# Weights stored by input channel instead of turned on TensorE, and a new order of the first two images

## The chip, the cores and the metric

One core of a Trainium2 chip runs the program. The metric is the device time of one execution in microseconds. The host's preparation of the inputs is not in it.

## What is computed

x is (8, 512, 32, 48) in float32, there are 40 centroids, W is 512 x 512.

```python
xn = x / max(norm(x, axis=1), EPS); cn = centroids / max(norm(centroids, axis=1), EPS)
idx = argmax(einsum('bchw,nc->bnhw', xn, cn), axis=1)          # nearest of 40 centroids
onehot = one_hot(idx, 40)
sum_x = einsum('bhwn,bchw->bnc', onehot, x)                     # cluster sums of each image
centroids_local = sum_x / max(count, 1)
gathered = centroids_local[b, idx]                              # mean of the pixel's cluster
delta = gathered - x
alpha = exp(-mean(delta * delta, axis=1))
y = x + alpha * delta
out = relu(einsum('oc,bchw->bohw', W, y) + b)
```

## The kernel before

An image has 1536 pixels, cut into three units of 512 pixels; units 0 to 23 run through the eight images. Channels are four blocks of 128 on the partitions. Each engine has its own program, written out by hand in order, and semaphores tie them together. Nothing reorders an engine's program: what stands behind a waiting instruction waits too.

For each unit `similarities(g)` (L915) multiplies x by the centroids. The result goes through ScalarE (`copy_sims`, L712) back to TensorE, `transpose_sims` (L924), and VectorE finds the maximum and the one-hot of all three units of an image in five instructions (`best_sims` and `first_best`, L425 to L440). `sum_clusters(b, u)` (L960) multiplies the one-hot by x with pixels on the partitions (the tile `xt`). `add_halves` (L970, L972) and a few small steps make the means G. `gather(g, h)` (L1000) multiplies the means by the one-hot, `delta(g, h)` (L483, VectorE) subtracts x, `square` (L673, ScalarE) squares, `add_chunks` adds the four channel blocks (for units 0 and 1 on GpSimd, L382 twice and L385 once), `sum_squares_direct(g)` (L1011) sums over partitions, `exp` (L688), `scale` (L519, VectorE, with `al` in PSUM), `y_half` (L527 on VectorE for unit 0, L360 on GpSimd for most others; both operands in SBUF), a high and a low part of y (L693, L367) and the product with the weights in three passes, `convolve` (L1023 to L1025; `high_passes`, L1084, for unit 0). The product of a unit comes two units after its gather.

x with pixels on the partitions comes in three ways. For image 1 (units 0 to 2) TensorE transposes it (`transpose_x`, L1037, 8 transposes of 128 x 128 a half unit) into the PSUM banks `gat` and `main`, and ScalarE (once VectorE) copies it out, `keep_transposed` (L655). Units 4 and 5 of image 2 are turned in the same way by `turn(step)` (L1055) and `keep_turned(step)` (L662); `TURNS` lists the steps and their tiles. All other units are loaded a second time as blocks of 32 channels (`load_xs`, L275, four loads a unit) and turned by VectorE, `transpose_half` (L411).

The weights are loaded once into the output buffer `OUT[0]` (L292). TensorE transposes them, `transpose_weights(k)` (L1077, 4 transposes each), into `gat` and `main`; `high_weights(k)` (L781, ScalarE) and `low_weights(k)` (L539, VectorE) split them into two parts. The squares of unit 0 use `OUT[0]` afterwards.

All loads and stores are issued by one queue, SP, in the order of its program. In what follows unit and image numbers are counted from 0 in the code; the text's "image 2" is b = 1, units 3 to 5.

Of the kernel before, what the change touches and what calls it, by code (L numbers as in the profile page):

```python
# [14 lines left out]
P = 128  # L15
# [27 lines left out]
TURNS = ((PARTS + 1, (0,)), (PARTS + 1, (1,)), (PARTS + 1, (2, 3)), (PARTS + 2, (0, 1)), (PARTS + 2, (2, 3)))  # L43
# [55 lines left out]
def build(nc, x, cent, w, bias, out):  # L99
# [3 lines left out]
    with ctx:  # L103
# [48 lines left out]
        cstat = sb("cstat", [P, 7], F32)  # L152
        Wraw = OUT[0]
# [31 lines left out]
        wT_ps, wh_done, wl_done = sem("wt_ps"), sem("wh_done"), sem("wl_done")  # L185
# [23 lines left out]
        def wT(k):  # L209
            return (gat[:, 0, :], gat[:, 1, :], main[:, 0, :], main[:, 1, :])[k]  # L210
# [51 lines left out]
        def _(sp):  # L262
# [33 lines left out]
            load_x(4)  # L296
            load_x(5)
            load_xs(3)
# [99 lines left out]
        def _(dve):  # L398
# [165 lines left out]
            low_weights(0)  # L564
            low_weights(1)
            low_clusters(0)
            counts(0)
            low_weights(2)
            rest_of_mean(0)
            parts_of_mean(0)  # L570
            low_weights(3)

            delta(0, 0)
            delta(0, 1)
            transpose_half(3, 0)
# [4 lines left out]
            transpose_half(3, 1)  # L580
# [69 lines left out]
        def _(act):  # L650
# [14 lines left out]
            def square(g, h):  # L665
                act.wait_ge(z_done, 2 * g + h + 1)
                if g < LAG:

                    act.wait_ge(wT_ps, KC)
                    act.wait_ge(const_done, 7)  # L670
                elif h == 0:
                    wait(act, s_done, folded(g - 1))
# [106 lines left out]
            def high_weights(k):  # L779
                act.wait_ge(wT_ps, k + 1)  # L780
# [3 lines left out]
            copy_sims(1)  # L784
            keep_transposed(0, 1)
            copy_sims(2)
# [4 lines left out]
            high_weights(0)  # L791
            high_weights(1)
            copy_onehot(0)
            copy_sums(0)
            evacuate_onehot()
            high_weights(2)
            scale_means(0)
            high_means(0)
            high_weights(3)
            keep_turned(0)  # L800
            act.wait_ge(b_in, 16)
            copy_sims(3)
            copy_sims(4)
# [3 lines left out]
            keep_turned(1)  # L807
            keep_turned(2)
            keep_turned(3)
            keep_turned(4)  # L810
# [81 lines left out]
        def _(pe):  # L892
# [43 lines left out]
            def sum_clusters(b, u):  # L936
# [4 lines left out]
                if PARTS * b + u in TURNED:  # L941
                    pe.wait_ge(xe_act, KEPT + 3 + 2 * TURNED.index(PARTS * b + u))
# [32 lines left out]
            def gather(g, h):  # L975
# [3 lines left out]
                if g == 0:  # L979

                    pe.wait_ge(wl_done, KC // 2 * (h + 1))
                    if h == 0:
                        pe.wait_ge(xe_act, KEPT + 1)
                elif g < LAG:

                    pe.wait_ge(xe_act, KEPT + 4 + h)
# [54 lines left out]
            def turn(step):  # L1041
                g, tiles = TURNS[step]
                if step == 0:

                    pe.wait_ge(wl_done, 1)
                elif step < 3:

                    pe.wait_ge(z_done, step)
                else:

                    pe.wait_ge(xe_act, KEPT + step - 1)
# [21 lines left out]
            def transpose_weights(k):  # L1073
# [124 lines left out]
```

## Time and profile before

| | us |
|---|---|
| median of 3 runs | 410.63 (409.59 to 411.04) |
| the profiled execution | 410.88 |
| its span, first to last instruction | 409.1 |
| TensorE busy | 403.9 |
| VectorE busy | 338.9 |
| GpSimd busy | 262.1 |
| ScalarE busy | 260.7 |
| granted TensorE clock | 0.999 |

The span is 1.8 us shorter than the execution. Times in the rows are from the span's start. TensorE's matmuls are pipelined, so a row's duration overlaps the next by 0.1 to 0.2 us; the chain of waits shows pieces without overlap.

### The profile page before, as it was taken

What the parts mean: (1) busy time and instruction counts of PE and PEld (TensorE: products, weight loads), DVE (VectorE), ACT (ScalarE), POOL (GpSimd) and SP (SyncE); (2) the same over time, 40 slices, a digit from 0 to 9 for tenths busy, and PEclk for the clock granted to TensorE, in tenths of its full rate; (3) what the DMA queues carried; (4) which work ended last, traced back from release to release, by engine and by line L of the source; (5) the groups of instructions that cost most, each with busy time, mean ns of one, the idle gap of its engine ahead of it and who ended that gap; (6) DMA issues with size and microseconds to landing.
All of it is one profiled execution on the core that took longest, in us unless ns stands there. A gap on an engine that the chain in (4) does not pass through costs nothing.

```text
span 409.1 us, 5812 instructions
## 1 busy us (share of the span) xinstructions
PE 403.9 (99%) x2088; PEld 288.2 (70%) x2088; DVE 338.9 (83%) x415; ACT 260.7 (64%) x362; POOL 262.1 (64%) x117
## 2 busy tenths in 40 slices
PE   8999999999999999999999999999999999999997
PEld 5746376775867677775867758776777758777886
DVE  2439999888899879999799898998799897898730
ACT  6566783767665684665865576656846658676641
POOL 2003773984599676994789946996769947433420
PEclk9999999999999999999999999999999999999999
DMA  7992493988499395967979575994957240222213
GB/s 256 380 248 51 88 244 84 297 252 180 172 246 266 113 281 140 272 162 183 265 198 229 191 163 188 254 256 118 276 139 226 104 129 13 103 103 104 103 68 138
DMA packets 77918, 74.51 MB, mean 182 GB/s; under 512 B 13723, under 2 KB 52891, under 8 KB 77891
## 3 DMA queue, kind: packets, MB, share of 16 engines
q1 hardware_dynamic: 77890, 74.15, 64.7%
q8 instruction: 17, 0.28, 0.3%
q14 instruction: 11, 0.08, 0.1%
HBM read 46.22 MB, written 25.17 MB: 174 GB/s over the span
## 4 chain that ended last, share of the span: by engine, by line
PE 95%; POOL 1%; DMA 1%; ACT 1%; issue 0%; DVE 0%; SPq 0%; ACTq 0%
PE main L1023 21%; PE main L1024 21%; PE main L1025 21%; PE fa L915 11%; PE sump L960 8%; PE gat L1000 5%; PE fa L924 1%; PE al L1006 1%; DMA x<-x 1%; PE main L1084 1%; PE main L1037 1%; PE al L1011 1%; POOL o L382 1%; POOL o L385 1%; PE gat L1037 1%; PE main L1055 0%
## 5 line engine op out<-in xcount | busy, mean ns | idle before, releaser
L1023 PE MATMUL main<-yh,wh 128*128 128x512 f32 (+1 forms) x376 | 152.8, 406 | 0.0
L1024 PE MATMUL main<-yl,wh 128*128 128x512 f32 (+1 forms) x376 | 146.3, 389 | 0.0
L1025 PE MATMUL main<-yh,wl 128*128 128x512 f32 (+1 forms) x376 | 146.1, 389 | 0.0
L360 POOL TENSOR_TENSOR z<-z,x 128x1024 f32<-128x1024 f32 x41 | 97.4, 2395 | 60.5 <-DVE z L519 60.5
L367 POOL TENSOR_TENSOR yl<-z,yh 128x1024 fp32r<-128x1024 f32 x43 | 103.7, 2429 | 13.8 <-ACT yh L693 13.7
L701 ACT ACTIVATE o<-main,bcol 128x512 f32<-128x512 f32 x96 | 65.1, 680 | 46.8 <-PE main L1025 45.9
L1023 PEld LDWEIGHTS main<-yh,wh 128*128 128x128 f32 x376 | 70.7, 188 | 21.4 <-issue 4.6
L1025 PEld LDWEIGHTS main<-yh,wl 128*128 128x128 f32 x376 | 70.6, 188 | 14.9
L1024 PEld LDWEIGHTS main<-yl,wh 128*128 128x128 f32 x376 | 70.7, 188 | 13.8
L374 POOL TENSOR_TENSOR xr<-xt 128x2048 f32<-128x2048 f32 x11 | 51.5, 4684 | 19.1 <-DVE xt L411 19.1
L483 DVE TENSOR_TENSOR z<-gat,x 128x1024 f32<-128x1024 f32 x46 | 55.8, 1213 | 6.1 <-PE gat L1000 6.1
L519 DVE TENSOR_TENSOR z<-z,al 128x1024 f32<-128x1024 f32 x48 | 56.3, 1210 | 0.6 <-ACT al L688 0.5
L693 ACT ACTIVATE yh<-z 128x1024 fp32r<-128x1024 f32 x48 | 50.6, 1053 | 3.6 <-POOL z L360 1.8
L915 PE MATMUL fa<-x,c_t 128*64 128x256 f32 x384 | 47.2, 394 | 0.5 <-DMA x<-x 0.5
L411 DVE STREAM_TRANSPOSE xt<-xs 128x1024 f32<-128x1024 f32 x38 | 46.1, 1225 | 0.0
L915 PEld LDWEIGHTS fa<-x,c_t 128*64 128x64 f32 x384 | 26.5, 140 | 19.3 <-issue 5.8
L673 ACT ACTIVATE sq<-z 128x1024 f32<-128x1024 f32 x21 | 22.3, 1060 | 25.7 <-DVE z L483 25.7
L673 ACT ACTIVATE gat<-z 128x1024 f32<-128x1024 f32 x21 | 21.5, 1024 | 25.2 <-DVE z L483 25.2
L419 DVE TENSOR_TENSOR xr<-xr 128x2048 bf16<-128x2048 f32 x11 | 36.7, 3338 | 0.2
L960 PE MATMUL sump<-xt,oh 128*64 128x512 f32 (+1 forms) x148 | 31.7, 537 | 0.0
L382 POOL TENSOR_TENSOR o<-o 128x512 f32<-128x512 f32 x4 | 5.1, 1284 | 36.2 <-ACT o L673 36.2
L1000 PE MATMUL gat<-oht,g 128*128 128x512 bf16 x92 | 27.8, 384 | 0.0
(139 smaller groups left out, 402.6 us busy)
## 6 DMA issues: line engine op xcount, KB each, us to landing
out<-o SPq DMA_DIRECT2D x23, 1024.0 KB, 7.2
x<-x SPq DMA_DIRECT2D x21, 1024.0 KB, 6.6
xs<-x SPq DMA_DIRECT2D x76, 256.0 KB, 5.5
x<-x SPq DMA_DIRECT2D x12, 256.0 KB, 5.4
o<-w SPq DMA_DIRECT2D x1, 1024.0 KB, 8.4
out<-o SPq DMA_DIRECT2D x3, 256.0 KB, 2.0
out<-o SPq DMA_DIRECT2D x2, 128.0 KB, 1.7
oht<-oh SPq DMA_TRANSPOSE x7, 3.7
```

Source lines behind the costliest of these rows:

```text
L360: pool.tensor_tensor(z, z, X[g // PARTS % 2][:, pair(h), span(g)], ALU.add).then_inc(y_pool, 1)
L367: pool.tensor_tensor(YL[g % 2][:, pair(h), :], Z[g % 2][:, pair(h), :], YH[g % 2][:, pair(h), :].bitcast(F32), ALU.subtract).then_inc(lo_p ...
L374: pool.tensor_tensor(XR[:, g % PARTS, :, :].rearrange("p t c -> p (t c)"), xt.rearrange("p t c -> p (t c)"), halfword(xt, 1), ALU.subtract ...
L483: v_.tensor_tensor(Z[g % 2][:, pair(h), :], banks(g, h)[:, :, :], X[g // PARTS % 2][:, pair(h), span(g)], ALU.subtract).then_inc(z_done, 1)
L519: v_.tensor_tensor(z, z, al[:, :].unsqueeze(1).to_broadcast([P, 2, UNIT]), ALU.mult).then_inc(za_done, 1)
L693: a_.activation(YH[g % 2][:, pair(h), :], Z[g % 2][:, pair(h), :], ACT.Copy).then_inc(hi_done, 1)
L701: a_.activation(OUT[g % 2][:, o, cols], main[:, o % 2, cols], ACT.Relu, bias=bcol[:, o:o + 1]).then_inc(relu_done, 1)
L915: last = t_.matmul(simP[u][NPAD * h:NPAD * (h + 1), :], cT[:, k, :], toks, start=(k == 0), stop=(k == KC - 1))
L960: last = t_.matmul(sumP[NPAD * h:NPAD * (h + 1), :], onehot[:, slot(u, tile), :], x_part[:, tile * C:(tile + 1) * C], start=(opens and t = ...
L1023: t_.matmul(tile, WH[:, k, rows], YH[g % 2][:, k, cols], start=(k == 0), stop=False)
L1024: t_.matmul(tile, WH[:, k, rows], YL[g % 2][:, k, cols], start=False, stop=False)
L1025: last = t_.matmul(tile, WL[:, k, rows], YH[g % 2][:, k, cols], start=False, stop=(k == KC - 1))
```

## The change

The host stores W transposed, so that what lands in `OUT[0]` is already laid out by input channel. `transpose_weights` goes, `wT(k)` names the landed rows, `high_weights` waits for the load itself, and its four calls move on ScalarE: the first stands between two evacuations of x. On TensorE the similarities of unit 2 move ahead of `transpose_x(0, 1)`, `transpose_sims(0)` ahead of `transpose_x(1, 0)`. The five turning steps become four of two tiles each, two of them ahead of the first gather. `sum_squares_direct(0)` moves behind `gather(1, 1)`. VectorE does the two halves of unit 3's transposes before and after the first two deltas, instead of later. SP loads unit 3's blocks ahead of unit 5.

```diff
-TURNS = ((PARTS + 1, (0,)), (PARTS + 1, (1,)), (PARTS + 1, (2, 3)), (PARTS + 2, (0, 1)), (PARTS + 2, (2, 3)))
+TURNS = ((PARTS + 1, (0, 1)), (PARTS + 1, (2, 3)), (PARTS + 2, (0, 1)), (PARTS + 2, (2, 3)))
...
         def wT(k):
-            return (gat[:, 0, :], gat[:, 1, :], main[:, 0, :], main[:, 1, :])[k]
+            return Wraw[:, k, :]
...
             load_x(4)
+            load_xs(3)
             load_x(5)
-            load_xs(3)
             load_xs(6)
...
             first_best(0)
-            low_weights(0)
-            low_weights(1)
+            for k in range(KC):
+                low_weights(k)
             low_clusters(0)
             counts(0)
-            low_weights(2)
             rest_of_mean(0)
             parts_of_mean(0)
-            low_weights(3)
-
+
+            transpose_half(3, 0)
             delta(0, 0)
             delta(0, 1)
-            transpose_half(3, 0)
+            transpose_half(3, 1)
             best_sims(1)
             first_best(1)
             delta(1, 0)
             delta(1, 1)
-            transpose_half(3, 1)
             scale(0, 0)
...
                 if g < LAG:
 
-                    act.wait_ge(wT_ps, KC)
+                    act.wait_ge(wl_done, KC)
...
             def high_weights(k):
-                act.wait_ge(wT_ps, k + 1)
+                act.wait_ge(w_in, 16)
                 a_.activation(WH[:, k, :], wT(k), ACT.Copy).then_inc(wh_done, 1)
...
-                if g == 0:
-
-                    pe.wait_ge(wl_done, KC // 2 * (h + 1))
-                    if h == 0:
-                        pe.wait_ge(xe_act, KEPT + 1)
-                elif g < LAG:
-
-                    pe.wait_ge(xe_act, KEPT + 4 + h)
+                if g < LAG:
+
+                    pe.wait_ge(xe_act, KEPT + 2 * g + h + 1)
...
-                if step == 0:
-
-                    pe.wait_ge(wl_done, 1)
-                elif step < 3:
-
-                    pe.wait_ge(z_done, step)
+                if step < 2:
+
+                    pe.wait_ge(xe_act, KEPT - 1 + step)
                 else:
 
-                    pe.wait_ge(xe_act, KEPT + step - 1)
+                    pe.wait_ge(z_done, step - 1)
...
-            def transpose_weights(k):
-                pe.wait_ge(w_in, 16)
-                pe.wait_ge(xe_act, 4 if k < 2 else 5)
-                for o in range(KC):
-                    last = t_.transpose(wT(k)[:, o * P:(o + 1) * P], Wraw[:, o, k * P:(k + 1) * P], ident[:, :])
-                last.then_inc(wT_ps, 1)
...
-        "w": np.ascontiguousarray(L0_conv_W),
+        "w": np.ascontiguousarray(np.asarray(L0_conv_W).T),
```

Where the instructions stand now. TensorE from the second similarities to the cluster sums of image 1, before (`x` is the image, `fa`, `gat` and `main` are PSUM banks, `o` the landed weights):

```order
L915 MATMUL fa<-x,c_t 64x256 x8
L1037 MATMUL main<-ident,x 128x128 x8
L915 MATMUL fa<-x,c_t 64x256 x8
L1037 MATMUL gat<-ident,x 128x128 x8
L924 MATMUL fa<-ident,sims 128x128 x6
L1037 MATMUL main<-ident,x 128x128 x8
L1037 MATMUL gat<-ident,x 128x128 x8
L1037 MATMUL main<-ident,x 128x128 x8
L1077 MATMUL gat<-ident,o 128x128 x8
L960 MATMUL sump<-xt,oh 64x512 x12
```

and after, where the same lines have other numbers:

```order
L913 MATMUL fa<-x,c_t 64x256 x16
L1030 MATMUL main<-ident,x 128x128 x8
L922 MATMUL fa<-ident,sims 128x128 x6
L1030 MATMUL gat<-ident,x 128x128 x8
L1030 MATMUL main<-ident,x 128x128 x8
L1030 MATMUL gat<-ident,x 128x128 x8
L1030 MATMUL main<-ident,x 128x128 x8
L958 MATMUL sump<-xt,oh 64x512 x12
```

The two similarities stand together, the transposed similarities come two steps sooner, and the eight weight transposes are gone.

TensorE from the first gather to the cluster sums of image 2, before:

```order
L1000 MATMUL gat<-oht,g 128x512 x2
L1000 MATMUL main<-oht,g 128x512 x2
L915 MATMUL fa<-x,c_t 64x256 x8
L1055 MATMUL gat<-ident,x 128x128 x4
L924 MATMUL fa<-ident,sims 128x128 x6
L1055 MATMUL main<-ident,x 128x128 x8
L1055 MATMUL gat<-ident,x 128x128 x8
L1055 MATMUL main<-ident,x 128x128 x8
L1000 MATMUL gat<-oht,g 128x512 x2
L1011 MATMUL al<-o,ones 128x512
L1000 MATMUL main<-oht,g 128x512 x2
L960 MATMUL sump<-xt,oh 64x512 x12
```

and after:

```order
L993 MATMUL gat<-oht,g 128x512 x2
L993 MATMUL main<-oht,g 128x512 x2
L913 MATMUL fa<-x,c_t 64x256 x8
L1045 MATMUL gat<-ident,x 128x128 x8
L922 MATMUL fa<-ident,sims 128x128 x6
L1045 MATMUL main<-ident,x 128x128 x8
L993 MATMUL gat<-oht,g 128x512 x2
L993 MATMUL main<-oht,g 128x512 x2
L1004 MATMUL al<-o,ones 128x512
L958 MATMUL sump<-xt,oh 64x512 x12
```

Twelve of the tile transposes now stand ahead of the first gather, and the sum of squares comes behind both gathers of unit 1.

VectorE from the argmax of image 2 to the y of unit 0, before:

```order
L440 TENSOR_TENSOR oh<-rank,fa 128x12x40
L483 TENSOR_TENSOR z<-gat,x 128x1024
L483 TENSOR_TENSOR z<-main,x 128x1024
L411 STREAM_TRANSPOSE xt<-xs 128x8x4x32
L519 TENSOR_TENSOR z<-z,al 128x1024
L527 TENSOR_TENSOR z<-z,x 128x1024
L519 TENSOR_TENSOR z<-z,al 128x1024
L527 TENSOR_TENSOR z<-z,x 128x1024
```

and after:

```order
L441 TENSOR_TENSOR oh<-rank,fa 128x12x40
L484 TENSOR_TENSOR z<-gat,x 128x1024
L484 TENSOR_TENSOR z<-main,x 128x1024
L520 TENSOR_TENSOR z<-z,al 128x1024
L528 TENSOR_TENSOR z<-z,x 128x1024
L520 TENSOR_TENSOR z<-z,al 128x1024
L528 TENSOR_TENSOR z<-z,x 128x1024
```

The block transpose between the deltas and the first scale is gone from here.

## Rows read from the trace of the kernel before

**Rows 1.** The page, part 4: the chain that ended last, shares by engine.
```profile
PE 95%; POOL 1%; DMA 1%; ACT 1%; issue 0%; DVE 0%; SPq 0%; ACTq 0%
```

**Rows 2.** TensorE's waits: total us, times, longest us.
```profile
PE al L1011 <- POOL o L385: 0.3, 1, 0.3
```

**Rows 3.** The chain, first 80 us: start us, us, engine, tile, line, count.
```profile
14.96 1.02 PE gat L1037 x8
15.99 0.66 PE fa L924 x6
...
17.55 1.03 ACT xt L655
...
18.63 1.10 PE main L1037 x8
19.73 0.97 PE gat L1077 x8
20.70 5.32 PE sump L960 x24
...
28.66 0.43 PE gat L1055 x4
...
33.70 1.88 PE fa L915 x16
...
36.16 0.86 PE fa L924 x6
```

**Rows 4.** Timeline, 40 to 48 us, all engines: start, us, engine, line, tiles, [idle before].
```profile
40.65 1.23 DVE L483 TENSOR_TENSOR z<-gat,x 128x1024 f32<-128x1024 f32 x1 [0.16 <-PE gat L1000]
...
41.94 1.22 DVE L483 TENSOR_TENSOR z<-main,x 128x1024 f32<-128x1024 f32 x1
...
42.00 2.26 ACT L673 ACTIVATE o<-z 128x1024 f32<-128x1024 f32 x2
...
43.13 2.53 POOL L382 TENSOR_TENSOR o<-o 128x512 f32<-128x512 f32 x2 [3.39 <-ACT o L673]
...
44.24 1.18 DVE L519 TENSOR_TENSOR z<-z,al 128x1024 f32<-128x1024 f32 x1
45.46 1.28 DVE L527 TENSOR_TENSOR z<-z,x 128x1024 f32<-128x1024 f32 x1
...
45.73 2.15 POOL L385 TENSOR_TENSOR o<-o 128x512 f32<-128x512 f32 x1
...
47.90 1.23 DVE L527 TENSOR_TENSOR z<-z,x 128x1024 f32<-128x1024 f32 x1
47.90 3.50 POOL L367 TENSOR_TENSOR yl<-z,yh 128x1024 fp32r<-128x1024 f32 x1
```

**Rows 5.** Timelines of GpSimd and of VectorE at 122 us.
```profile
121.89 2.39 POOL L367 TENSOR_TENSOR yl<-z,yh 128x1024 fp32r<-128x1024 f32 x1
124.24 5.97 POOL L374 TENSOR_TENSOR xr<-xt 128x2048 f32<-128x2048 f32 x1
...
122.59 4.20 DVE L419 TENSOR_TENSOR xr<-xr 128x2048 bf16<-128x2048 f32 x1
```

**Rows 6.** Timeline of SP's queue: issues of weights, unit 5, unit 3's fourth block.
```profile
7.33 0.53 SPq L292 DMA_DIRECT2D o<-w  x1
...
12.09 1.22 SPq L268 DMA_DIRECT2D x<-x  x1
...
21.30 1.30 SPq L275 DMA_DIRECT2D xs<-x  x1
```

**Rows 7.** DMA issues at 6.8, 7.3, 12.1, 21.3 us: KB each, us from issue to landing.
```profile
x<-x SPq DMA_DIRECT2D x1, 256.0 KB, 6.1
...
o<-w SPq DMA_DIRECT2D x1, 1024.0 KB, 8.4
...
x<-x SPq DMA_DIRECT2D x1, 1024.0 KB, 13.6
...
xs<-x SPq DMA_DIRECT2D x1, 256.0 KB, 9.4
```

More of the change, by code:

```diff
@@ L184, in build @@
         cT_ps, cT_done, norm_step = sem("ct_ps"), sem("ct_done"), sem("norm_step")
-        wT_ps, wh_done, wl_done = sem("wt_ps"), sem("wh_done"), sem("wl_done")
+        wh_done, wl_done = sem("wh_done"), sem("wl_done")
         xp_done, xe_dve, xe_act = sem("xp_done"), sem("xe_dve"), sem("xe_act")
@@ L784, in _ @@
             copy_sims(1)
+            copy_sims(2)
             keep_transposed(0, 1)
-            copy_sims(2)
+            high_weights(0)
             keep_transposed(1, 0)
@@ L790, in _ @@
             keep_transposed(2, 1)
-            high_weights(0)
             high_weights(1)
             copy_onehot(0)
+            high_weights(2)
+            high_weights(3)
             copy_sums(0)
             evacuate_onehot()
-            high_weights(2)
             scale_means(0)
             high_means(0)
-            high_weights(3)
             keep_turned(0)
@@ L802, in _ @@
             copy_sims(3)
+            keep_turned(1)
             copy_sims(4)
@@ L806, in _ @@
             square(0, 1)
-            keep_turned(1)
             keep_turned(2)
             keep_turned(3)
-            keep_turned(4)
             exp(0)
@@ L941, in sum_clusters @@
                 if PARTS * b + u in TURNED:
-                    pe.wait_ge(xe_act, KEPT + 3 + 2 * TURNED.index(PARTS * b + u))
+                    pe.wait_ge(xe_act, KEPT + 2 + 2 * TURNED.index(PARTS * b + u))
                 elif b > 0:
@@ L1089, in _ @@
             similarities(1)
+            similarities(2)
             transpose_x(0, 1)
-            similarities(2)
+            transpose_sims(0)
             transpose_x(1, 0)
-            transpose_sims(0)
             transpose_x(1, 1)
@@ L1096, in _ @@
             transpose_x(2, 1)
-            transpose_weights(0)
-            transpose_weights(1)
             pe.wait_ge(const_done, 7)
@@ L1103, in _ @@
             transpose_onehot()
-            transpose_weights(2)
-            add_halves(0)
-            transpose_weights(3)
             pe.wait_ge(x_in[1][1], 16)
             turn(0)
+            add_halves(0)
+            turn(1)
             similarities(3)
@@ L1113, in _ @@
             similarities(5)
-            turn(1)
+            turn(2)
             transpose_sims(1)
-            turn(2)
             turn(3)
-            turn(4)
             gather(1, 0)
+            gather(1, 1)
             sum_squares_direct(0)
-            gather(1, 1)
             sum_clusters(1, 1)
@@ L1127, in _ @@
             pe.wait_ge(z_done, 4)
+            pe.wait_ge(wl_done, KC)
             pe.wait_ge(hi_done, 1)
```

## The prediction

> **What bounds the kernel now.** Read the chain of waits first: TensorE carries 95% of the span [rows 1]. Then the list of TensorE's own waits: it is short, and its last entry in time is 0.3 us in front of `sum_squares_direct(1)`, for GpSimd's last chunk sum [rows 2], whose matmul starts at 48.01. After that TensorE waits for nothing to the end, so whatever shift `sum_squares_direct(1)` has is the shift of the whole kernel. The change lies entirely ahead of that point. The question is therefore not how many matmuls go, but when that one instruction starts. I walk the first 48 us engine by engine, in order, with the durations of the rows; each instruction keeps the order that the changed program gives it.
>
> **Removed: the 16 weight transposes (L1077).** Eight cost 0.97 us on the chain at 19.73; four fill the 0.44 from 28.22 to the row at 28.66 [rows 3]. The other four lie in the stretch in which TensorE waits for the high and low parts of the cluster sums, so they cost nothing. That is 1.41 us on the chain. The four copies of weight rows on ScalarE and the four subtractions on VectorE remain, with SBUF as the source in place of PSUM. I take the same 0.6 and 0.7 us for them. Except for the first one on ScalarE they fall into the 5.32 us of `sum_clusters(0, *)` [rows 3], where both engines have room. If SBUF made them twice as long they would still end about when `sum_clusters` does, at 25. The new waits for the low weights (first square on ScalarE, `high_passes` on TensorE) come 9 us and more after that and cost nothing.
>
> **Moved: the similarities of unit 2 ahead of `transpose_x(0, 1)`.** They start at 12.06 instead of 13.09. Their last slice of x, issued at 6.8, lands 6.1 us later at 12.9 [rows 7]. It is wanted at 12.06 plus three quarters of 1.9, so 13.5. No wait. They end at 13.94, the transposes of x at 14.98, and `transpose_sims(0)` at 15.64 where it was 16.65 (the row at 15.99 and its 0.66) [rows 3]. VectorE's argmax follows about 1.0 earlier.
>
> **Added: `high_weights(0)` in front of `keep_transposed(1, 0)` on ScalarE.** `keep_transposed(0, 1)` starts at 15.02 when its transposes end and takes 1.03 like its sister at 17.55 [rows 3]; ScalarE can take the next at about 15.95, a little before it ends. The weights are issued at 7.33 and land 8.4 later, at 15.7 [rows 6, 7], just before. The copy delays the next evacuation by 0.48. That evacuation ends at 17.60, and `transpose_x(2, 0)`, which refills the bank, starts at 17.64. Before, the last pair of x transposes waited for ScalarE in the same way and started at 18.63 [rows 3]. Now TensorE runs 1.10 + 0.97 from 17.64 and begins `sum_clusters` at 19.71, where it began at 20.70: **0.99 earlier**. So 0.97 of transposes gone, and the 1.0 of the reordering spent again on ScalarE.
>
> **Moved: the turned tiles of image 2.** `turn(0)` and `turn(1)` (8 transposes each, 0.93 and 0.90) now stand before and after `add_halves(0)`. `sum_clusters` and the one-hot transposes end at 25.69, `turn(0)` at 26.62. Before, `add_halves` (0.7) ended at 28.22, so it started at 27.52, 1.5 after the end of `sum_clusters` at 26.02, because its inputs came then; now they come at 25.03 + 1.5 = 26.5, and the turn covers it. `add_halves` and `turn(1)` end at 28.22. Before, the similarities of unit 3 began when the row at 28.66 ended, 29.10 [rows 3]: 0.88 earlier. From 29.10 to 36.16 TensorE did similarities, two gathers, the last similarities (1.88 from 33.70) and four tile transposes, 7.06 us [rows 3]. Now there are eight tile transposes in place of four, 0.37 more (0.95 against 0.58). Then six transposes at 0.68, which before took 0.86 since ScalarE's copy came late; the free ones at 15.99 took 0.66 [rows 3]. They end at 36.33 against 37.02: **0.69 earlier**. Twelve tile transposes of the 32 leave the stretch behind this point, so TensorE itself gains 1 us more there; VectorE does not.
>
> **Moved: unit 3's blocks.** The fourth block load of unit 3 is issued at 21.30 and lands at 30.7; unit 5, in front of it, is issued at 12.09 and lands at 25.7 [rows 6, 7]. Unit 5 is wanted by `similarities(5)`, 0.88 before the 33.70 of rows 3. The gathers begin 1 us before that, at 31.8, and `transpose_half(3, 0)` stands on VectorE between the means and the deltas, so it wants the blocks at about 31.4. In the new order the two exchange places: blocks at about 28, unit 5 at about 30.7. Both have 2 us or more. The transpose costs VectorE 0.1 us against `delta(0, 0)`, which has 1 us of room before `turn(2)` needs it.
>
> **The step that decides.** The argmax of image 2 ends 3.47 us after the transposed similarities (37.02 to 40.49, where VectorE went idle for 0.16) [rows 3, 4], so now at 39.80, and `delta(1, 0)` starts there: 0.85 earlier than 40.65. `delta(1, 1)` follows at 40.94, `scale(0, 0)` at 42.08 (steps of 1.14, as from 41.94 through the block transpose to 44.24, and that transpose is gone), `y_half(0, 0)` 1.22 later at 43.30 [rows 4]. ScalarE's square starts 0.02 after the delta's 1.23 and takes 1.06, so GpSimd's first chunk sum of unit 1 runs from 42.18 to 43.46. The second, 1.27, would run to 44.73 and the third to 46.1. `sum_squares_direct(0)`, moved behind `gather(1, 1)`, is done before the argmax is, so its move costs nothing. TensorE arrives at `sum_squares_direct(1)` at 45.76 (it starts `sum_clusters(1, 1)` at 39.90, when the one-hot is there, and 5.32 + 0.54 follow), so it would run at 46.2: the gain would be 1.8.
>
> The trace says that GpSimd does not run freely beside this VectorE instruction. The third chunk sum took 2.15 instead of 1.27. It was to start at 45.73, while `y_half(0, 0)` ran from 45.46; 45.46 + 1.28 = 46.74, and 46.74 + 1.14 = 47.88, its end [rows 4]. `y_half(0, 1)` and the low half on GpSimd both began at 47.90; VectorE took 1.23, GpSimd 3.50 instead of 2.39, which is again VectorE's end plus a run [rows 4, 5]. While VectorE scaled by a PSUM operand (44.24) GpSimd lost nothing. And when VectorE waits behind one GpSimd instruction and another stands right behind it, VectorE goes between: L419 issued at 122.59 waited for the end of L367 at 124.28, and L374, issued at 124.24, ended at 130.21, 3.4 after L419's end at 126.79 [rows 5].
>
> With that in the walk: `y_half(0, 0)` waits for 43.46 and ends at 44.54; the second sum ends at 45.68; `scale(0, 1)` from 44.46; `y_half(0, 1)` wants the port at 44.46 + 1.24 = 45.70, the third sum at 45.68 + 0.07 = 45.75. VectorE is ahead by 0.05 and runs to 46.93; the third sum ends at 48.07; TensorE starts 0.12 later at 48.19. **That is 0.18 us later than 48.01**: all that the change removes is waited for again, 2.4 us long, at `sum_squares_direct(1)`.
> The Trainium skill (SBUF — State Buffer, Who interferes with whom) says of a VectorE instruction with two SBUF inputs and a GpSimd instruction that reads SBUF that whichever is issued first has the port for all of its run. The rows agree, and by that rule too the order 45.70 before 45.75 decides; with the order turned round the time would be the second case below.
>
> **Sum.** Span 409.1 + 0.18 = 409.3. The profiled execution took 410.88, 0.25 above the median of 410.63; on the median's footing the forecast is **410.8**. Behind `sum_squares_direct(1)` every wait hangs on ScalarE's exp, which hangs on it, so the pattern moves as a whole.
>
> **Rivals.**
> (B) GpSimd gets one of the two turns. My walk is good to about 0.1 us, and the margins are 0.16 and 0.05. Then the third sum ends at 46.95 (43.46 + 1.27, 1.08 of VectorE, 1.14), TensorE at 47.1: 0.9 earlier, 409.7. For it: the thin margin. Against it: rows 4 show the same race at 47.90 with VectorE winning.
> (C) The removed work comes through whole: TensorE at 46.2, 408.8. It takes a GpSimd that is not held up at all; two rows speak against it.
> (D) Slower: the weights land late. ScalarE stands in order at `high_weights(0)`, with four evacuations of x behind it that TensorE waits for. From a landing at 16.0 on, each us of lateness is one us for TensorE. Other 1 MB loads of this queue land up to 13.6 after issue [rows 7] instead of 8.4; with a latency of 10.4, 2 us more, the weights come at 17.7 and the kernel is at about 412.5. Against it: nothing ahead of them in the queue changes.
> (E) The change doesn't do what it says on the clock because unit 5 lands late: pushed behind the blocks it may mix with unit 6's and come at 33 to 34; one us late is one us, about 411.8.
>
> **Chances.** The forecast 0.52, B 0.20, C 0.13, D 0.08, E 0.07. A measurement of this kernel can tell about 0.3% (1.2 us) from no change. Faster by more: C and a third of B and a little of the forecast, 0.23. Slower by more: D, half of E and a little of the forecast, 0.14. Within: 0.63. The range 409.0 to 412.2 leaves out C and the far end of D, and holds the spread of the runs.
>
> **What would show it.** TensorE's waits: `sum_squares_direct(1)` for GpSimd, about 2.4 us (forecast), 1.3 (B), 0.4 (C). The chunk sums of unit 1: second and third over 2 us each (forecast), one of them (B), none (C). `sum_clusters(0, 0)` starting at 19.7; if it starts later, a wait of ScalarE for the weights (D). The similarities of unit 5 waiting for a DMA (E). The forecast is wrong if TensorE waits less than 1 us in front of `sum_squares_direct(1)`.

## The result: slower by 0.6%, and the profile after

| | before | after |
|---|---|---|
| median of 20 executions, us | 410.44 | 412.90 |
| lowest to highest, us | 409.59 to 411.05 | 410.62 to 416.83 |
| after / before, 95% interval | | 1.0062 (1.0049 to 1.0075) |
| profiled execution, us (its span) | 410.88 (409.1) | 412.77 (411.0) |
| executions with a mean granted clock below 0.999 | 0 of 20 | 14 of 20 |

The forecast was 410.8 in a range of 409.0 to 412.2, with "within 0.3%" the likeliest. The median lies 2.1 us above the forecast and outside the range, on the side that I gave 14 in 100. The spread has changed too: before, all executions lie within 1.5 us of each other, after, within 6.2.

The list of TensorE's waits of the profiled execution of after (total us, times, longest us), which answers to [rows 2]:

```profile
PE al L1004 <- POOL o L386: 2.2, 1, 2.2
PE fa L913 <- DMA x<-x: 1.5, 1, 1.5
PE al L1052 <- POOL ones L335: 1.0, 1, 1.0
PE gat L1030 <- ACT xt L654: 0.9, 1, 0.9
PE main L993 <- ACT xt L661: 0.6, 1, 0.6
```

The first is the wait that the forecast names, at `sum_squares_direct(1)` (L1004). The second is rival E, the similarities of unit 5. The third is the start and was there before. The chain that ended last has lost seven points of TensorE against [rows 1] to SP's queue and the DMAs, which is unit 5's way into the chip:

```profile
PE 88%; SPq 5%; DMA 3%; POOL 1%; DVE 1%; issue 0%; ACT 0%
```

The same execution in its timeline, 16 to 50 us, TensorE, VectorE, ScalarE and GpSimd mixed (start, us, engine, line, tiles, idle before and who ended it). These rows answer to [rows 3, 4]:

```profile
16.44 0.63 ACT L780 ACTIVATE wh<-o 128x512 fp32r<-128x512 f32 x1 [0.61 <-DMA o<-w]
18.04 1.09 PE L1030 MATMUL gat<-ident,x 128*128 128x128 f32 x8 [0.86 <-ACT xt L654]
19.98 5.37 PE L958 MATMUL sump<-xt,oh 128*64 128x512 f32 x24
28.36 3.67 PE L913 MATMUL fa<-x,c_t 128*64 128x256 f32 x32
34.55 1.95 PE L913 MATMUL fa<-x,c_t 128*64 128x256 f32 x16 [1.55 <-DMA x<-x]
41.56 1.22 DVE L484 TENSOR_TENSOR z<-gat,x 128x1024 f32<-128x1024 f32 x1
...
43.95 3.51 POOL L383 TENSOR_TENSOR o<-o 128x512 f32<-128x512 f32 x2 [3.29 <-ACT o L672]
45.07 1.25 DVE L528 TENSOR_TENSOR z<-z,x 128x1024 f32<-128x1024 f32 x1
46.24 1.21 DVE L520 TENSOR_TENSOR z<-z,al 128x1024 f32<-128x1024 f32 x1
47.48 1.22 DVE L528 TENSOR_TENSOR z<-z,x 128x1024 f32<-128x1024 f32 x1
47.54 2.29 POOL L386 TENSOR_TENSOR o<-o 128x512 f32<-128x512 f32 x1
49.88 1.12 PE L1004 MATMUL al<-o,ones 128*128 128x512 f32 x2 [2.21 <-POOL o L386]
```

Read the lower half first, since it is the step on which the forecast was built. From `delta(1, 0)` to `sum_squares_direct(1)` the walk had 39.80 to 48.19, 8.39 us; the trace has 41.56 to 49.88, 8.32. GpSimd's first two chunk sums of unit 1 took 3.51 together, where the pair took 2.53 before [rows 4]: the second was held up. The third took 2.29: it stands behind `y_half(0, 1)` (47.48), which came 0.06 us before the third sum's start (47.54); the walk said 0.05. The whole of it stands 1.7 us later than forecast, and 1.55 of that is the wait at 34.55 for unit 5. The span of this execution, 411.0, is the forecast's 409.3 plus the same 1.7. So the profiled execution has one fault of the forecast in it. Its granted clock is 1.0 throughout, so what the 14 executions with a lower clock lose doesn't show in it.

Every sign that the forecast named for itself is there: a wait of 2.2 us at `sum_squares_direct(1)`, and the second and third chunk sums over 2 us each (3.51 less a free one of 1.27 is 2.24, and 2.29). The time is wrong all the same.

### The profile page after: what moved, and what is told of

The parts are those of the page before. It is cut to its first block, busy times and chain, and to the rows that moved or that the text cites. A ratio compares the mean times of both kernels' runs of the same rounds, so it can differ in the third digit from the quotient of the medians.

```text
span 411.0 us, 5770 instructions
## 1 busy us (share of the span) xinstructions
PE 401.5 (98%) x2068; PEld 286.3 (70%) x2072; DVE 338.3 (82%) x415; ACT 260.5 (63%) x361; POOL 262.2 (64%) x117
## 4 chain that ended last, share of the span: by engine, by line
PE 88%; SPq 5%; DMA 3%; POOL 1%; DVE 1%; issue 0%; ACT 0%
PE main L1016 21%; PE main L1017 21%; PE main L1018 21%; PE fa L913 8%; PE sump L958 7%; PE gat L993 5%; DMA x<-x 3%; SPq L276 2%; SPq L292 1%; PE al L999 1%; PE fa L922 1%; PE main L1067 1%; POOL o L383 1%; SPq L269 1%; POOL o L386 1%; PE al L1004 0%
## 5 line engine op out<-in xcount | busy, mean ns | idle before, releaser
L368 POOL TENSOR_TENSOR yl<-z,yh 128x1024 fp32r<-128x1024 f32 x43 | 102.6, 2402 | 14.8 <-ACT yh L692 14.8
L520 DVE TENSOR_TENSOR z<-z,al 128x1024 f32<-128x1024 f32 x48 | 56.5, 1219 | 2.9 <-ACT al L687 2.9
L383 POOL TENSOR_TENSOR o<-o 128x512 f32<-128x512 f32 x4 | 6.1, 1526 | 37.0 <-ACT o L672 37.0
L993 PE MATMUL gat<-oht,g 128*128 128x512 bf16 x88 | 26.9, 384 | 0.5 <-issue 0.3
```

Source lines behind the costliest of these rows:

```text
L368: pool.tensor_tensor(YL[g % 2][:, pair(h), :], Z[g % 2][:, pair(h), :], YH[g % 2][:, pair(h), :].bitcast(F32), ALU.subtract).then_inc(lo_p ...
L520: v_.tensor_tensor(z, z, al[:, :].unsqueeze(1).to_broadcast([P, 2, UNIT]), ALU.mult).then_inc(za_done, 1)
```

## Experiments

Ratios are to the kernel before, run beside each, with 95% intervals. My theory after the result had two parts. (1) Unit 5 lands late and by a varying amount, which costs what it is late. (2) The wait of 2.2 us at `sum_squares_direct(1)` makes TensorE's granted clock fall, which costs more than the wait. The rival to (2) is that the low clocks come from the wait for unit 5, or from outside. The rival to the lock as such is that GpSimd's chunk sums are merely longer there, whatever VectorE does.

**The loads in their old order.** This edit of the kernel after, "loads back", is also the base of seven later runs. (The expectations call the runs of this section e1 to e4, f1 to f4, g1 to g3 and h1, in this order.)

```
             load_x(4)
-            load_xs(3)
             load_x(5)
+            load_xs(3)
```

> The changed kernel with one part undone: unit 5 is loaded ahead of unit 3's blocks again. Theory 1 (two causes: unit 5's late landing costs 1.55 us, GpSimd's chunk sums beside VectorE's y_half cost the rest): the wait of the similarities of unit 5 (1.55 us) goes, the wait of sum_squares_direct(1) for GpSimd stays at about 2.2 us, sum_squares_direct(1) starts at 48.3 instead of 49.88, and the kernel takes 410.7 us, ratio 1.000 to 1.001. The spread of its runs falls from 6 us to that of before, 1.5 us. Theory 2 (the load order is not the cause, the slowdown lies in the chunk sums or behind 50 us): it stays at 412.5 to 413.

Measured: 412.13 us, ratio 1.0046 (1.0029 to 1.0062). A miss of the expectation by 1.4 us, and the most telling one. In its profile TensorE waits for no DMA. Of the seven executions two have a clock of 0.999 or 1.0, with spans of 408.8 and 408.7; the five others have 0.995 or 0.996 and spans of 410.1 to 411.2. There is nothing between. The profiled one is of the first kind, and it is the kernel that the forecast describes, 0.5 us below the span of 409.3: `sum_clusters(0, 0)` starts at 19.28 instead of the walk's 19.71, `sum_squares_direct(1)` at 47.57 instead of 48.19. With unit 5 loaded in its old place the low clocks are still there, so they don't need the wait for it.

**Without the port.** The loads back, and `y_half(0, 0)` adds a tile from PSUM in place of x, so that this VectorE instruction has only one operand in SBUF. Left out: unit 0's first half of y is not the reference's.

```
                 z = Z[g % 2][:, pair(h), :]
-                v_.tensor_tensor(z, z, X[g // PARTS % 2][:, pair(h), span(g)], ALU.add).then_inc(y_dve, 1)
+                other = X[g // PARTS % 2][:, pair(h), span(g)]
+                if (g, h) == (0, 0):
+                    other = al[:, :].unsqueeze(1).to_broadcast([P, 2, UNIT])
+                v_.tensor_tensor(z, z, other, ALU.add).then_inc(y_dve, 1)
```

> As e1, and y_half(0, 0) on VectorE adds the PSUM tile al instead of x, same size (so unit 0's first half of y is not the reference's). Theory (GpSimd is held up since that instruction reads two SBUF operands): the chunk sums of unit 1 take 1.27 us each up to the third, y_half(0, 1) waits for the third instead; the wait of sum_squares_direct(1) falls from 2.2 to about 0.4 us, it starts at 46.4, and the kernel takes 408.8 us, 1.9 less than e1. Rival (GpSimd is slow there for another reason, such as ScalarE's traffic or its own queue): no difference from e1, 410.7 us.

Measured: 408.5 us, ratio 0.9966 (0.9953 to 0.9979), all five clocks 1.0, 0.3 below the expectation; the start that was expected at 46.4 is at 45.50. The list of waits has no entry for GpSimd at `sum_squares_direct(1)`. Its timeline at the same place:

```profile
41.56 2.52 POOL L383 TENSOR_TENSOR o<-o 128x512 f32<-128x512 f32 x2 [3.18 <-ACT o L675]
42.69 1.22 DVE L531 TENSOR_TENSOR z<-z,al 128x1024 f32<-128x1024 f32 x1
44.16 1.28 POOL L386 TENSOR_TENSOR o<-o 128x512 f32<-128x512 f32 x1
45.08 1.45 DVE L531 TENSOR_TENSOR z<-z,x 128x1024 f32<-128x1024 f32 x1
45.50 1.12 PE L1007 MATMUL al<-o,ones 128*128 128x512 f32 x2
```

The VectorE row at 42.69, the one with the PSUM operand, runs inside the first GpSimd row and neither is longer than alone. The sums take 2.52 and 1.28 instead of 3.51 and 2.29. So the 2.2 us come from this instruction's second operand in SBUF, the rival of merely long sums falls, and what the change removes does come through (rival C's 408.8) when the lock is gone. The Trainium skill (SBUF — State Buffer, Who interferes with whom) ties the sharing to both inputs being in SBUF, and the row with one PSUM input agrees.

**A different order on VectorE.** The loads back, and `transpose_half(3, 1)` again behind `delta(1, 1)`, so that VectorE stands 1.2 us later at its first y half:

```
             delta(0, 1)
-            transpose_half(3, 1)
...
             delta(1, 1)
+            transpose_half(3, 1)
             scale(0, 0)
```

> As e1, and the second half of unit 3's block transpose stands again between delta(1, 1) and scale(0, 0) on VectorE. Theory (where y_half falls against the chunk sums decides): y_half(0, 0) starts 1.2 us later, so that only the third chunk sum is held up, as in the kernel before; wait of sum_squares_direct(1) about 1.3 us, start at 47.4, kernel 409.8 us, 0.9 less than e1, although VectorE has more to do there. Rival (VectorE's work in that stretch is what is late, more of it makes it worse): 410.7 us or up to 1.2 more.

Measured: 409.51 us, ratio 0.999 (0.9981 to 0.9998), as expected to 0.3. GpSimd's pair takes 2.54 and the third sum 2.13, one hold-up instead of two, and TensorE waits 0.95:

```profile
46.56 1.10 PE L1004 MATMUL al<-o,ones 128*128 128x512 f32 x2 [0.95 <-DVE z L520]
```

The profile puts this wait down to VectorE's `scale(0, 1)` (L520), which ends at 46.42; the third chunk sum ends at 46.41. The two end together, so GpSimd alone doesn't set the start any more. All eleven clocks are 1.0, the first sign that the shorter wait spares the clock.

**One chunk sum less.** The loads back, and TensorE adds the two halves itself for unit 1, with two accumulating products, so that GpSimd's third sum isn't needed:

```
+                if g == 1:
+                    return
                 pool.wait_ge(two_done, 2 * g + 2)
...
+                if g == 1:
+                    for h in range(2):
+                        pe.wait_ge(two_done, 3 + h)
+                        last = t_.matmul(al[:, :], ones[:, :].bitcast(F32), squares(g, h)[:, 0, :],
+                                         start=(h == 0), stop=(h == 1))
```

> As e1, and unit 1's third chunk sum on GpSimd is left out: sum_squares_direct(1) adds its two halves itself with two accumulating matmuls. TensorE gets 0.9 us more work. Theory: the first starts when the second chunk sum ends, about 46.0, the second ends at 48.0 instead of 49.4, kernel 409.3 us, 1.4 less than e1. Rival (TensorE's time counts more than the wait): 410.7 us or 0.9 more.

Measured: 409.23 us, ratio 0.9988 (0.9978 to 0.9998), all eleven clocks 1.0, no wait at this place. TensorE pays 0.8 us for the added products (1.88 instead of 1.1). As expected (409.3). In this execution it also waited 0.8 for ScalarE at `transpose_x(2, 0)`, and VectorE 0.71 for unit 3's blocks.

**The kernel after once more**, unchanged, to get a trace of an execution with a low clock.

> The changed kernel as it is, for another trace. In 15 of its 20 executions the mean granted TensorE clock was 0.999 or lower, mostly 0.995 or 0.996, in the kernel before it was 0.999 to 1.000; the profiled execution had 1.000. Theory 1 (the waits of TensorE around 34 us and 49 us make the chip grant the lower clock for some us after them): where an execution has 0.995 its trace shows a stretch of granted clock under 1.00 that begins shortly behind one of the two waits, and matmuls of twice the length in it; it costs about 2 us. Theory 2 (the lower clock has another origin): the stretch lies elsewhere.

Measured: 412.13 us, ratio 1.0054 (1.0022 to 1.0086). The expectation counts 15 executions of after with a clock of 0.999 or lower; it is 16, and 14 of them are below 0.999. Here five of the eight executions have a clock of 0.991 to 0.996, and the profiled one is among them (span 410.6, clock 0.995). It has no wait for unit 5 at all, so it shows the clock alone. By windows (length, then busy us of PE, PEld, DVE, ACT and POOL with their counts, granted clock, DMA share, GB/s):

```profile
46.00:48.00 2.00, 0.00 (x0) 0.00 (x0) 1.53 (x2) 0.26 (x1) 2.00 (x1) 0.99 1.02 194
48.00:50.00 2.00, 1.89 (x3) 0.86 (x4) 0.00 (x0) 0.00 (x0) 2.00 (x2) 0.50 1.08 238
50.00:52.00 2.00, 2.00 (x7) 1.60 (x6) 1.17 (x1) 1.78 (x3) 0.51 (x2) 0.65 1.20 218
52.00:54.00 2.00, 2.00 (x10) 1.63 (x9) 1.75 (x3) 1.71 (x3) 2.00 (x1) 1.00 1.11 279
```

TensorE does nothing in the first window. In the second its clock is 0.50, that is 1.2 GHz instead of 2.4, in the third 0.65 on the mean, then 1.00 again. TensorE's timeline there:

```profile
48.11 2.07 PE L1004 MATMUL al<-o,ones 128*128 128x512 f32 x2 [2.20 <-POOL o L386]
49.20 1.42 PE L1067 MATMUL main<-yh,wh 128*128 128x512 f32 x1
50.41 0.63 PE L1067 MATMUL main<-yh,wl 128*128 128x512 f32 x1
...
54.32 0.40 PE L968 MATMUL fa<-sums_h,select 128*128 128x512 f32 x1
```

and the same instructions with the loads back, in an execution at full clock:

```profile
47.57 1.12 PE L1004 MATMUL al<-o,ones 128*128 128x512 f32 x2 [2.19 <-POOL o L386]
48.13 0.80 PE L1067 MATMUL main<-yh,wh 128*128 128x512 f32 x1
48.76 0.39 PE L1067 MATMUL main<-yh,wl 128*128 128x512 f32 x1
...
52.28 0.40 PE L968 MATMUL fa<-sums_h,select 128*128 128x512 f32 x1
```

The wait is the same, 2.20 and 2.19. `sum_squares_direct(1)` starts at 48.11 here, where the forecast had 48.19. But its two products take 2.07 instead of 1.12, and from its start to L968 it is 6.21 us instead of 4.71: 1.5 us lost. The spans are 1.8 apart (410.6 and 408.8), of which 0.5 was there already at `sum_clusters(0, 0)` (19.81 and 19.28).

**The wait filled.** The loads back, and eight products of 128 columns in front of `sum_squares_direct(1)`, into a bank that is free there, whose values nothing reads. They shorten no wait of another engine; they only keep TensorE busy.

```
             gather(2, 0)
+            pe.wait_ge(z_done, 4)
+            for _ in range(8):
+                t_.matmul(main[:, 0, 0:P], ones[:, :].bitcast(F32), ones[:, :].bitcast(F32), start=True, stop=True)
             sum_squares_direct(1)
```

> As e1 (unit 5 loaded ahead of unit 3's blocks), and TensorE runs eight dummy 128x128 float32 products, about 2.0 us, into a free bank in the 2.2 us in which it waits for GpSimd. Nothing is computed sooner. e1's executions came in two groups: spans of 408.7 to 408.8 at clock 0.999 to 1.000 (2 of 7) and 410.1 to 411.2 at 0.995 to 0.996 (5 of 7). Theory 1 (the idle stretch makes the clock fall): all executions at 0.999 or more, median 410.5 instead of 412.1, although TensorE has 2 us more to do. Theory 2 (the clock falls for other reasons): the same two groups, median 412.

Measured: 410.63 us, ratio 1.0007 (0.9997 to 1.0016), as expected, with all eleven clocks at 1.0. `sum_squares_direct(1)` starts at 47.69, 0.12 later than with the loads back, behind products that end 0.4 before it:

```profile
45.35 1.95 PE L1106 MATMUL main<-ones 128*128 128x128 f32 x16
47.69 1.12 PE L1004 MATMUL al<-o,ones 128*128 128x512 f32 x2 [0.39 <-POOL o L386]
```

Work that is of no use, ends nothing sooner and starts nothing sooner makes the kernel faster by 1.5 us at the median (412.13 to 410.63). At full clock the profiled executions of the two kernels have the same span, 408.8, and over all executions the clock is what sets them apart: below 0.999 in 5 of 7 and in 0 of 11. This is also the kernel that the forecast had in mind: same order, same wait, no fall of the clock, 0.2 us below the 410.8.

**The weights alone.** The kernel before with the weights by input channel (turned by the host, as in the change), without the 16 transposes, with the semaphore waits that hung on them moved over, and every other thing in its old place:

```
-                return (gat[:, 0, :], gat[:, 1, :], main[:, 0, :], main[:, 1, :])[k]
+                return Wraw[:, k, :]
...
-            transpose_weights(0)
-            transpose_weights(1)
...
-            transpose_weights(2)
...
-            transpose_weights(3)
```

> The kernel before with one part of the change alone: weights laid out by input channel, no weight transposes on TensorE, everything else in the order of before (unit 4's and 5's turning steps, block transposes, loads, ScalarE's order). Theory (the removed transposes are worth what the argmax and the means leave of them): sum_clusters(0, 0) starts 0.5 earlier, when the one-hot is there, the first gather 0.8 earlier, and since VectorE, ScalarE and GpSimd keep their order up to sum_squares_direct(1), that starts 0.8 earlier too: 409.4 to 409.6 us, ratio 0.998. Rival (the gain is waited for again at sum_squares_direct(1), as in the changed kernel): 410.2 us, no difference.

Measured: 409.69 us, ratio 0.9984 (0.9975 to 0.9993), 0.1 above the expectation. Half of the removed 1.41 us comes through at the median. Its waits show where the rest went: 0.7 us in front of `add_halves(0)` for VectorE's low parts of the cluster sums, where it was 0.3 before, 0.5 at the head of the cluster sums, and 0.4 in front of the first gather for VectorE's means.

**The best of the parts so far:** the loads back, `transpose_half(3, 1)` back, the two accumulating products, and `high_weights(0)` behind the last evacuation of x on ScalarE.

```
             keep_transposed(0, 1)
-            high_weights(0)
...
+            high_weights(0)
             high_weights(1)
```

> A candidate: as e3 (unit 5 loaded first, the second block transpose back behind delta(1, 1)), with e4's two matmuls in place of the third chunk sum of unit 1, and high_weights(0) on ScalarE behind the last evacuation of x instead of ahead of the second. The wait of TensorE for ScalarE at transpose_x(2, 0), 0.2 to 0.9 us in the runs so far, goes; sum_squares_direct(1) does not wait. Sum: e3's 409.5 less 0.2 (two matmuls end 0.15 earlier than wait and one) less 0.2 to 0.4 (ScalarE): 409.0 us, ratio 0.997 to 0.998, all executions at full clock. If TensorE's order before the argmax of image 2 isn't what counts, 409.3 to 409.5.

Measured: 409.92 us, ratio 0.9986 (0.9977 to 0.9995). A miss by 0.9 us. With GpSimd's third sum gone, `sum_squares_direct(1)` waits for VectorE's `scale(0, 1)` (L522), which takes its columns out of the bank that the products write:

```profile
45.91 1.98 PE L1008 MATMUL al<-o,ones 128*128 128x512 f32 x4 [0.87 <-DVE z L522]
```

I had asked only which engine makes the inputs of this instruction, and not who still reads the tile it writes.

**The landing alone.** The kernel after with its own load order, and the same eight products in the wait, so that the clock is held and unit 5 can be late:

> The changed kernel with its own load order (unit 5 behind unit 3's blocks), and the eight dummy products in TensorE's wait for GpSimd. Theory (three separate terms: the wait for GpSimd itself, the clock that falls behind it, unit 5's late landing): the clock term goes and the landing term stays: granted clock 0.999 to 1.000 in nearly all executions, median 410.6 to 411.5 (f2's 410.6 plus 0 to 2 us of lateness), above f2 and below the changed kernel's 412.9, spread over 2 us. If the lower clock comes from the wait for unit 5 as well, some executions stay at 0.995.

Measured: 412.22 us, ratio 1.0051 (1.0029 to 1.0074). That is 0.7 above the top of the median's expected range, 410.6 to 411.5. Seven of the eight clocks are 1.0 now, and still the spans reach from 408.9 to 411.8 (and 412.6 at the one clock of 0.996). Against the same kernel with the loads back (410.63, ratio 1.0007, 0.8 us from lowest to highest) the order of the loads costs 1.6 to 1.8 us at the median, and nearly all of the spread.

**The kernel before with only its load order changed:**

> The kernel before with the load order alone changed: unit 3's blocks ahead of unit 5. There the similarities of unit 5 begin at 33.70; behind the blocks unit 5 landed at 31.7 in one trace of the changed kernel and at 34.5 in the other. Theory (the landing is late in some executions): no cost in half of them, up to 0.8 us in the others, median 410.4 to 410.8 against 410.2, highest 411.5 to 412. Rival (the order of loads is free in the order of before since everything wanted has 2 us of room): no difference in median nor in spread.

Measured: 410.91 us (409.56 to 414.83), ratio 1.0021 (1.0001 to 1.0041). The median is 0.1 above the expectation, the highest execution 2.8 above it. The cost, barely clear of noise, is less than in the kernel after, which fits that before wants unit 5 later (33.70 at the earliest, not 32.8). But the spread comes with it: spans of 407.8 to 410.4, and one of 413.0. The similarities of unit 5 wait in its profile:

```profile
34.90 1.95 PE L915 MATMUL fa<-x,c_t 128*64 128x256 f32 x16 [0.64 <-DMA x<-x]
```

Why unit 5 is late can be read from the queue of SP in the kernel after (start and us of the issues of unit 3's four blocks, of unit 5, and of unit 6's four blocks):

```profile
12.26 7.85 SPq L276 DMA_DIRECT2D xs<-x  x4
20.16 3.78 SPq L269 DMA_DIRECT2D x<-x  x1
23.98 5.72 SPq L276 DMA_DIRECT2D xs<-x  x4
```

and from the times to landing of unit 5 (issued at 20.16) and of the first of unit 6's blocks (issued at 23.98):

```profile
x<-x SPq DMA_DIRECT2D x1, 1024.0 KB, 14.3
xs<-x SPq DMA_DIRECT2D x1, 256.0 KB, 9.0
```

Unit 5 lands at 34.5 and the first block of unit 6 at 33.0, though it was issued 3.8 us behind it. In the four traces with this order unit 5 landed at 31.7, 33.3, 34.5 and 34.9. In the ten traces with unit 5 in its old place the load took 13.3 to 15.7 us, so it isn't slower behind the blocks; it is issued 8 us later, at 19.2 to 20.2 instead of 11.6 to 12.1. The Trainium skill (DMA: Bandwidth & Descriptors, Queues, rings and completion order) says that completion isn't first in, first out for an issuing engine: a copy is split over several of the 16 DMA engines, and a later copy's completion says nothing of the other engines of an earlier one. The two landings agree.

**A candidate without the moved transpose:** the loads back, the two accumulating products, `high_weights(0)` late, and `transpose_half(3, 1)` where the change puts it.

> A candidate: the changed kernel with unit 5 loaded first, the third chunk sum of unit 1 replaced by a second accumulating matmul, and high_weights(0) behind the last evacuation of x on ScalarE. Against f4 VectorE's second block transpose stays ahead of the argmax, so that scale(0, 1), for which sum_squares_direct(1) waited 0.9 us in f4, ends 1.1 us sooner. Against e4 TensorE no longer waits for ScalarE at transpose_x(2, 0) (0.8 us in e4's trace). Sum: e4's 409.2 less 0.3 to 0.5: 408.8 us, ratio 0.997. If f4's 409.9 was due to high_weights(0)'s new place and not to scale(0, 1): 409.5 or more.

Measured: 409.36 us, ratio 0.9979 (0.9968 to 0.9991). Faster than before, but 0.6 short of the expectation, and the reason is in VectorE's timeline:

```profile
32.33 1.25 DVE L414 STREAM_TRANSPOSE xt<-xs 128x1024 f32<-128x1024 f32 x1 [1.26 <-DMA xs<-x]
```

In this execution unit 3's blocks, loaded in the old order, come too late for the place to which the change moves their transpose. VectorE stands 1.26 us, `turn(2)` on TensorE 0.5. It varies: with the same loads and the same transpose in this place VectorE stood 0.71 us with the two accumulating products and 0.45 with `transpose_half(3, 1)` back, and not at all in three more traces (loads back, PSUM operand, filled wait). So the change of the load order had a ground: in some executions the blocks are late in the one order, in some unit 5 in the other.

**Both put right in the order of VectorE:** the candidate before, with `transpose_half(3, 0)` behind `delta(0, 1)` and `transpose_half(3, 1)` behind `delta(1, 1)`, where they wait for nothing, and `scale(0, 1)` ahead of `y_half(0, 0)`, so that the bank of `al` is read before `sum_squares_direct(1)` wants it.

```
-            transpose_half(3, 0)
             delta(0, 0)
             delta(0, 1)
-            transpose_half(3, 1)
+            transpose_half(3, 0)
...
             delta(1, 1)
+            transpose_half(3, 1)
             scale(0, 0)
-            y_half(0, 0)
             scale(0, 1)
+            y_half(0, 0)
             y_half(0, 1)
```

> A candidate from the two misses: f4 (loads, both matmuls, weights late on ScalarE) with both block transposes where the kernel before has them, so that VectorE no longer stands in front of delta(0, 0) for unit 3's blocks (1.26 us in g3), and with scale(0, 1) ahead of y_half(0, 0), so that sum_squares_direct(1) no longer waits for it (0.87 us in f4). TensorE's waits at sum_squares_direct(1) and turn(2) both go. f4's 409.9 less 0.9: 409.0 us, ratio 0.997, all executions at full clock. If y_half(0, 0), now 1.2 us later, makes high_passes wait for ScalarE's high part, the gain shrinks to 0.3: 409.6.

Measured: 409.29 us (408.95 to 409.47), ratio 0.9972 (0.9961 to 0.9983), clocks 0.999 to 1.0. It is faster than both kernels, 0.3% below before, with a spread of 0.5 us in seven executions. The products of unit 1 wait for nobody; `high_passes` behind them waits 0.3 for ScalarE's high part, a part of what the expectation feared:

```profile
44.67 1.88 PE L1008 MATMUL al<-o,ones 128*128 128x512 f32 x4
```

## Why the prediction was wrong, step by step

**Removed transposes, moved similarities.** Right in size: 0.97 and 0.44 us are gone from TensorE. That not all of it comes through is confirmed by the weights alone, which bring 0.7 of 1.41.

**`high_weights(0)` ahead of `keep_transposed(1, 0)`.** The mechanism was right, the price too small in this execution. The weights landed at 16.4 (7.19 and 9.2) and not 15.7, and ScalarE stood 0.61 us. From the end of the early similarities to `sum_clusters(0, 0)` it was 6.30 us (13.68 to 19.98), where the walk had 5.77 and the filled wait and the second trace of after 5.68. This is rival D at a third of its price. TensorE's wait in front of `transpose_x(2, 0)` was 0.9 here, 0.4 with the loads back and 0.2 in the second trace of after. None of it is taken up by the later wait of 2.2 us: from `sum_clusters(0, 0)` to `sum_squares_direct(1)` it is 28.3 us with the loads back, with the wait filled and in the second trace of after, and 29.9 here, 1.6 more, which is the wait for unit 5. The sums on GpSimd hang on the same chain, so the wait moves along. The walk had 28.48.

**Turned tiles, similarities of unit 3.** Forecast 28.22, measured 28.36, with `sum_clusters` 0.27 later than in the walk. Right.

**Unit 3's blocks and unit 5. The first step that failed:** "the two exchange places: blocks at about 28, unit 5 at about 30.7. Both have 2 us or more." The last block landed at 29.6 (18.15 and 11.4), unit 5 between 31.7 and 34.9, with 32.8 as the time at which it is wanted. I took the landing of a block (9.4 after its issue) for that of a load four times its size, and the order of issue for the order of arrival. Rival E named the mixing with unit 6's blocks, the landing at 33 to 34 and the price; its chance of 0.07 was the error. The rows of before had the better number: unit 5's own load took 13.6 in its old place [rows 7], and 13.6 from the 20.2 at which it was issued in the new one is 33.8.

**The decisive step: port and wait.** Right to 0.1 us in the place that decides (8.32 against 8.39), in the wait (2.2 against 2.4), and in who wins which turn. `sum_squares_direct(1)`, forecast at 48.19, starts at 48.11, 47.57 and 47.69 where unit 5 is in time; the last two executions were 0.3 to 0.4 ahead of the walk already at `sum_clusters(0, 0)`. The margin of the second turn was 0.05 us, by the prediction's own words less than the walk's error, so calling it was partly luck; the race itself comes out alike in all five traces with this order, with 3.51 or 3.52 for the pair and 2.29 for the third sum. The run with the PSUM operand shows that the port is the cause, and rivals B and C are excluded as long as it is there.

**Behind it. The second step that failed:** "Behind `sum_squares_direct(1)` every wait hangs on ScalarE's exp, which hangs on it, so the pattern moves as a whole." Every instruction stands in the same pattern, but the pattern runs at another clock. The wait of 0.3 us before [rows 2] became 2.2, and in 14 of 20 executions the mean granted clock is below 0.999; in the one of that kind that was traced (0.995) it fell to 0.50 behind this wait and was back at 1.00 by 52, some 3.5 us later. I had priced the wait as the time by which things start later, and not as time in which TensorE does nothing. A fall of the clock was in none of the rivals and had no chance. That no execution of before shows a fall of the clock proved nothing, since before has no wait of that length: its longest behind the first microsecond is 0.5 us.

**The two together.** On top of the forecast pattern (ratio 1.0007) the clock costs 0.39% (loads back against filled wait) and the landing 0.44% (filled wait with the loads of after against loads back), 1.6 and 1.8 us. Their sum, 3.4, is more than the 1.9 to 2.3 us by which the kernel after lies above the forecast pattern (ratios 1.0054 and 1.0062 against 1.0007). The excess of 1.1 us (3.4 less 2.3) is itself good to about 1.3 by the intervals of the four ratios (an estimate), so it may be noise; whether the parts add up stays open. An execution in which unit 5 is late might be less prone to the fall of the clock, and the one traced with such a wait is at 1.0, but seven others with spans over 411.5 us, where unit 5 was probably late, have low clocks as well. Why the clock falls in two of three executions and not in all with the same wait, 2.20 and 2.19 us, is open too. So is the far end of the spread: 413.6 to 415.0 of span with clocks of 0.991 or 0.992, of which no trace was taken.

**Sum.** The shortest executions of after, at clocks of 0.999 or 1.0, have spans of 408.8 to 409.3 (five of the 28); the forecast was 409.3. The forecast describes that execution. It is the fastest kind, and not the median one. The two steps that failed, the landing of unit 5 and the clock behind the wait, are what the median has on top.

## What to carry to other kernels

A stall of the engine that bounds the kernel has two prices: the time, and on TensorE what the clock loses behind it. When a saving upstream is "only waited for again", look at how long the new wait is: here waits of 0.4 and 0.95 us never lowered the clock, and one of 2.2 us cost another 1.5 in most executions. Where the wait can't be removed, products that nobody reads can fill it. Such a wait isn't slack: what came late ahead of it came late behind it by the same amount.

Before two loads are exchanged, work out when each is wanted and when it lands by the time that a load of its own size, at that place in the queue, took; keep some us of room, and look at the spread of the executions as well as the median.

Where GpSimd works for the bounding engine, VectorE instructions with both inputs in SBUF belong behind its last sum. Or take the sum to TensorE, and then see who still reads the bank that the result goes to.

## What the runs showed of the hardware

- The granted clock fell from 1.0 to 0.50 behind one TensorE wait of 2.2 us in one trace; the mean granted clock was below 0.999 in 5 of 7 executions (loads back), 14 of 20 and 5 of 8 (after), and in none of 11 with the same wait filled by products. In the kernels with waits of at most 0.95 us at this place and unit 5 loaded in its old place it stayed at 0.999 or above in all executions. Of the kernels with late loads two had one execution each of 0.996, 1 of 8 with the wait filled and 1 of 12 with only the loads exchanged; their spans, 412.6 and 413.0, are the longest of their kernel, as a long wait for unit 5 would make them. Neither was traced, so whether such a wait lowers the clock is not shown; the longest traced one, 1.55 us, left it at 1.0.
- A load of 1 MB behind four of 256 KB on SP's queue took 12.5 to 14.8 us to land (13.3 to 15.7 ahead of them), and in three of four traces landed 1.4 to 2.2 us behind a block issued 3.8 to 4.1 us after it. Its issue took 3.6 to 4.1 us of SP's queue at 19 to 20 us, and 1.0 to 1.3 at 12 us.
- VectorE with both inputs in SBUF goes between two GpSimd instructions that stand back to back (3.51 for the pair instead of 2.52), and with one input in PSUM it runs beside them at no cost.
